# Linear attention between two mixture layers: 32 slots in a row instead of a loop of turns, x kept on chip, no identity products in front of the 64x64 groups

## The reference, cut to what matters

```python
x = x + 0.5 * ffn(layernorm(x))          # mixture layer, stage f1
x = x + linear_attention(layernorm(x))   # the part that changes
x = x + 0.5 * ffn(layernorm(x))          # mixture layer, stage f2

def step(carry, inp):                    # scan over 8 segments of 64 positions
    mem, z = carry
    q_s, k_s, v_s = inp
    sq = elu(q_s) + 1.0
    att_mem = sq @ mem / (sq @ z)
    sk = elu(k_s) + 1.0
    mem = mem + einsum('bhlk,bhlv->bhkv', sk, v_s)
    z = z + sk.sum(over the segment)
    att_dot = softmax(einsum('bhik,bhjk->bhij', q_s, k_s) * scale)
    att = gate * att_mem + (1.0 - gate) * (att_dot @ v_s)
```

## Time and profile before

| | |
|---|---|
| median of 3 runs | 2392.57 us |
| the profiled execution, its own time | 2382.67 us |
| its span, first to last instruction | 2381.0 us |
| attention stage | 844.4 to 1470.8 us |
| seven turns (b = 0 to 6), first `score` to first `score` | 70.3, 72.4, 74.9, 74.5, 72.4, 71.3, 69.0 us |
| last turn (b = 7) to the store's end | 59.1 us |

### The profile page before, as it was taken

How to read it: one execution, slowest core, us unless ns; L and a number is a source line. 1 busy time by engine, 2 the same in 40 slices (tenths; PEclk the granted TensorE clock), 3 DMA queues, 4 the chain that set the end, 5 groups by cost and what they waited for, 6 DMA issues and landing times. The chain is left out here.

```text
span 2381.0 us, 41513 instructions
## 1 busy us (share of the span) xinstructions
PE 1916.0 (80%) x12512; PEld 1065.6 (45%) x12513; DVE 1488.0 (62%) x3530; ACT 935.8 (39%) x1694; POOL 553.3 (23%) x640
## 2 busy tenths in 40 slices
PE   1899999998499958887888884599999998499940
PEld 1433333332299925565555663223333332189930
DVE  1678888884345437656666653487888886345533
ACT  0156666667222223332333321036666666322200
POOL 2222333311322231111001000222233331222246
PEclk9899999999699978888988986679999999799975
DMA  8336333320122231111011003335333330022245
GB/s 186 62 56 130 65 65 62 58 45 11 53 73 73 70 121 36 54 54 53 12 45 54 28 19 67 81 65 128 66 69 57 63 59 12 27 79 73 72 131 180
DMA packets 163076, 161.68 MB, mean 68 GB/s; under 512 B 20620, under 2 KB 153484, under 8 KB 162572
## 3 DMA queue, kind: packets, MB, share of 16 engines
q1 hardware_dynamic: 122048, 107.34, 19.7%
q10 hardware_dynamic: 30636, 27.21, 4.2%
q0 software_dynamic: 10240, 25.18, 3.7%
HBM read 90.80 MB, written 62.39 MB: 64 GB/s over the span
## 5 line engine op out<-in xcount | busy, mean ns | idle before, releaser
L576 DVE TENSOR_REDUCE f_M<-bank 128x1 f32<-128x512 f32 x1024 | 673.8, 685 | 194.0 <-PE bank L846 184.1
L486 ACT ACTIVATE f_PT<-bank 128x512 f32<-128x512 f32 x1024 | 573.0, 596 | 296.8 <-PE bank L863 292.2
L846 PE MATMUL bank<-f_KS,f_QS 96*128 96x512 bf16 x1024 | 403.8, 400 | 75.1 <-DVE f_M L576 39.1
L863 PE MATMUL bank<-f_QS,f_KS 99*128 99x512 bf16 x1024 | 394.8, 390 | 45.4 <-ACT f_PT L486 31.3
L863 PEld LDWEIGHTS bank<-f_QS,f_KS 99*128 99x128 bf16 x1024 | 99.9, 99 | 423.0 <-ACT f_PT L486 304.9
L873 PE MATMUL bank<-f_PT,f_V 128*32 128x512 f32 x2048 | 273.2, 607 | 0.0
L846 PEld LDWEIGHTS bank<-f_KS,f_QS 96*128 96x128 bf16 x1024 | 100.8, 99 | 204.8 <-DVE f_M L576 137.0
L1107 PE MATMUL bank<-f_room,f1m_gT 128*128 x568 | 136.2, 383 | 0.1
L1107 PE MATMUL bank<-f_room,f2m_gT 128*128 x568 | 135.3, 381 | 0.1
L415 POOL DMA_INDIRECT routed_rows<-f_AO,f_rows_i x128 | 124.7, 974 | 42.0 <-issue 42.0
L1107 PEld LDWEIGHTS bank<-f_room,f1m_gT 128*128 128x128 f32 x568 | 103.6, 193 | 11.8 <-issue 0.5
(11 more groups left out here) (257 smaller groups left out, 3027.4 us busy)
## 6 DMA issues: line engine op xcount, KB each, us to landing
f_QS<-q_parts SPq DMA_DIRECT2D x192, 64.0 KB
f_KS<-k_parts SPq DMA_DIRECT2D x168, 64.0 KB
expert_rows<-f1m_y ACTq DMA_DIRECT2D x71, 128.0 KB, 1.7
expert_rows<-f2m_y ACTq DMA_DIRECT2D x71, 128.0 KB, 1.7
xr<-f_xr SPq DMA_DIRECT2D x16, 512.0 KB, 3.0
f_room<-in_L_ffn_w SPq DMA_DIRECT2D x2, 4096.0 KB, 22.4
q_parts<-f_q SPq DMA_DIRECT2D x16, 384.0 KB, 2.5
k_parts<-f_k SPq DMA_DIRECT2D x16, 384.0 KB, 2.5
```

Of the source, the lines that this page charges most:

```text
L486: act.activation(PT[:, i % 8, :], SCE[i % 2][:, :], ACT.Exp).then_inc(probs_ready, 1)
L576: dve.tensor_reduce(M[:, t, h:h + 1], SCM[(a * SC + i) % 3][:, :], AX.X, ALU.max).then_inc(scm_drained, 1)
L846: pe.matmul(SCM[(a * SC + i) % 3][:, :], QS[par][0:K_MAX, h, t * P:(t + 1) * P], KS[par][0:K_MAX, h, :], start=True, stop=True).then_inc(s ...
L863: pe.matmul(SCE[i % 2][:, :], KS[par][0:K_EXP, h, t * P:(t + 1) * P], QS[par][0:K_EXP, h, :], start=True, stop=True).then_inc(sce_filled, 1)
```

## The change

- One slot per tile and no loop: 37 slots in a row (`SLOTS`), of which 4 only make the first batch's items, 32 have a tile and 1 closes; a batch is 4 slots, and its items are spread over them at four places A to D. The memory items stand with the items they need, and the last (`LATE`) in the first slot of its own batch. The layer norm of batch b+2 is made in four parts, one in each slot.
- PSUM is dealt out anew: `score` and `recall` share a pair of banks, the probabilities have two banks of their own, `OB` only the output, and the ring has 3 banks instead of 2.
- x stays in SBUF in 4 buffers: no store to `x_mid`, no load of it; `put_out` adds into the buffer.
- `carry` is gone.
- Keys are projected before queries; the gate is applied as (memory - attention) x gate + attention, with no `omg`.

Its core (the first `slot` is TensorE's, the second VectorE's):

```diff
-    PLACES = [[("hsT", 0), ("hsT", 1)], [("qk", 0), ("qk", 1)], [("qk", 2), ("qk", 3)], [("qk", 4), ("qk", 5)],
-              [("qk", 6), ("qk", 7)], [("v", 0), ("v", 1)], [("v", 2), ("v", 3)], [("sk", 0), ("sk", 1)],
...
+    PLACES = [{"A": [("hsT", 0), ("hsT", 1)], "B": [("qk", 0)], "C": [("qk", 1)], "D": [("qk", 2)]},
+              {"A": [("qk", 3), ("qk", 4)], "B": [("v", 0)], "C": [("v", 1)], "D": [("sk", 0)]},
...
-        SC, AMB, LB, OB, RING = bank[0:2], bank[2:4], bank[4], bank[5], bank[6:8]
+        SA, LB, OB, RING = bank[0:2], bank[2:4], bank[4], bank[5:8]
...
+            def slot(b, t):
+                g, before = tile(b, t), tile(b, t - 1)
+                if g is not None:
+                    score(g)
+                if before is not None:
+                    weigh(before)
+                make(b, t, "A")
+                if g is not None:
+                    recall(g)
+                make(b, t, "B")
+                if g is not None:
+                    turn_probabilities(g)
+                if before is not None:
+                    turn_out(before)
+                make(b, t, "C")
+                if before is not None:
+                    project_out(before)
+                make(b, t, "D")
...
+            def add_up(g):
-                s.own(dve.tensor_tensor(AL[:, :], LB, w["omg"][:, :], ALU.mult))
-                dve.tensor_tensor(AT[:, :], AM[:, t % 2, :], AL[:, :], ALU.add).then_inc(at_ready, 1)
+                own(dve.tensor_tensor(AT[:, :], AM[:, g % 2, :], LB[0], ALU.subtract))
+                own(dve.tensor_tensor(AT[:, :], AT[:, :], w["gate"][:, :], ALU.mult))
+                dve.tensor_tensor(AT[:, :], AT[:, :], LB[0], ALU.add).then_inc(at_ready, 1)
...
+            def slot(b, t):
+                g, before = tile(b, t), tile(b, t - 1)
+                last = ((b, t - 1) if t else (b - 1, T - 1)) if (b, t) != SLOTS[0] else None
+                if g is not None:
+                    subtract_maximum(g)
+                if last is not None:
+                    lows(*last, "D")
+                    memories(*last, "D")
+                if before is not None:
+                    add_up(before)
+                if last is not None:
+                    features(*last, "C")
+                memories(b, t, "A")
+                if g is not None:
+                    probabilities(g)
+                if last is not None:
+                    features(*last, "D")
+                lows(b, t, "A")
+                if g is not None:
+                    from_memory(g)
+                features(b, t, "A")
+                lows(b, t, "B")
+                if b + 2 < B:
+                    prepare_batch(b + 2, t)
+                features(b, t, "B")
+                lows(b, t, "C")
+                memories(b, t, "C")
+                if before is not None:
+                    put_out(before)
...
-                pe.matmul(free[:, 510:512], ident_b[:, :], ident_b[:, 0:2], start=True, stop=True)
```

More of the change, by code:

```diff
@@ L1607, in _, with score @@
             dve.wait_ge(gate_step, 2)
-            dve.tensor_scalar(w["omg"][:, :], w["gate"][:, :], -1.0, 1.0, ALU.mult, ALU.add).then_inc(gate_step, 1)
-            dve.wait_ge(gate_step, 3)
-            s = Steps(dve, dve_front, 0, FRONT)
-            for stage in (combine_rows, variance, normalise):
-                stage(0, s)
-            run_turns(dve, turn)
+            for b, t in SLOTS:
+                slot(b, t)
         @block.tensor
         def _(pe):
-            def carry(free):
-                pe.matmul(free[:, 510:512], ident_b[:, :], ident_b[:, 0:2], start=True, stop=True)
+            def score(g):
+                n = g // T
+                wait(pe, am_read, g)
+                if g % T == 0:
+                    pe.wait_ge(drained["qk"], (n + 1) * QK)
+                for h in range(H):
+                    pair, one = h // 2, h % 2
+                    part = slice(one * DK, (one + 1) * DK)
+                    for half in range(2):
+                        at = (2 * (g % T) + half) * LSEG
+                        seg = slice(at, at + LSEG)
+                        last = pe.matmul(SA[one][half * LSEG:(half + 1) * LSEG, pair * LSEG:(pair + 1) * LSEG],
+                                         qk[n % 2][part, pair, seg], qk[n % 2][part, PAIRS + pair, seg], start=True, stop=True)
+                last.then_inc(s_filled, 1)
@@ new lines, in recall @@
+            def recall(g):
+                n, t = divmod(g, T)
+                pe.wait_ge(s_ready, g + 1)
+                if t == 0:
+                    pe.wait_ge(sqk_ready, (n + 1) * QK)
+                pe.wait_ge(drained["mem"], n * U + 2 * t + 1)
+                for h in range(H):
+                    pair, one = h // 2, h % 2
+                    part = slice(one * DK, (one + 1) * DK)
+                    for half in range(2):
+                        seg = slice((2 * t + half) * LSEG, (2 * t + half + 1) * LSEG)
+                        last = pe.matmul(SA[one][half * LSEG:(half + 1) * LSEG, pair * VW:(pair + 1) * VW],
+                                         sqk[n % 2][part, pair, seg], MEM[n % 2][part, 2 * t + half, pair, :], start=True, stop=True)
+                last.then_inc(am_filled, 1)
@@ new lines, in turn_probabilities @@
+            def turn_probabilities(g):
+                pe.wait_ge(pb_ready, g + 1)
+                for half in range(2):
+                    if half == 0:
+                        wait(pe, at_ready, g)
+                    else:
+                        wait(pe, pbT_ready, g * 2)
+                    for i in range(PAIRS):
+                        last = pe.transpose(LB[half][:, i * P:(i + 1) * P], PB[g % 2][:, half * PAIRS + i, :], ident[:, :])
+                    last.then_inc(pbT_filled, 1)
@@ L1622, in turn_out, with weigh @@
+            def weigh(g):
+                pe.wait_ge(pbT_ready, (g + 1) * 2)
+                n, t = divmod(g, T)
+                for h in range(H):
+                    last = pe.matmul(LB[0][:, h * DK:(h + 1) * DK], PBT[:, (h % 2) * PAIRS + h // 2, :],
+                                     V[n % 2][:, t, h, 0:DK], start=True, stop=True)
+                last.then_inc(l_filled, 1)
             def turn_out(g):
                 pe.wait_ge(at_ready, g + 1)
+                wait(pe, y_ready, g)
@@ L1749, in _ @@
             pe.wait_ge(init, INIT)
             pe.wait_ge(la_loaded, 80)
-            run_turns(pe, turn)
+            for b, t in SLOTS:
+                slot(b, t)
 def macaron(nc, x, Wq, Wk, Wv, betas, Wo, q_w, q_b, k_w, k_b, v_w, v_b, o_w, o_b,
```

493 lines of the change are left out of this document (206 added, 287 removed), and 2 rows, old and new, of the table PLACES.

## The result

The changed kernel takes 2291.39 us (median of 4 runs, 2288.74 to 2299.78) and the one before 2391.93 (4 runs): a ratio of 0.9592, interval 0.9557 to 0.9627, about 98 us less by the ratio (the two medians are 100.5 apart). It was forecast 2326, in a range from 2284 to 2368. The sign, the range and the place of the gain were right; the gain itself was half as large again as the forecast's.

What follows compares the result with a forecast made beforehand. TensorE's work, its waits and its low clock were taken as the bound. Lead-in 26, first items 34.6, seven batches at 62.3 and last batch 69.3 made 566.0 against 626.4 us; forecast 2326, range 2284 to 2368.

Steps and rivals of the forecast that it cites:

- the last batch: Final tile slots, closing slot and store: nothing fills the waits, so 69.3 us against 59.1 before.
- Loop: Where the old loop goes back TensorE stands still: 5.5 us once, and its turns some 3 us longer.
- Identities: The 120 products ahead of 64x64 groups, 15 per batch, removed: 1.4 us a batch.
- x on chip: One store and two loads per batch become one load and one store; transfers hidden, counted 0.
- Gate: Three VectorE passes as before, but all behind `weigh`, one more than before: +0.69 us in the chain.
- The clock: Waits in third and fourth slots can lower TensorE's clock, 1.6 us a fall; 2.2 us a batch added.
- The walk: Four slots of a batch followed on the engines: 60.1 us at full clock, 52.1 work and 8.0 waits.
- Lead-in and first items: Attention's start before the seven batches: lead-in 25.0 to 26 us, first batch's items 37.4 to 34.6.
- the floor: Rival, 10%: waits shrink as products run into the next slot, clock stays up; batch 54 us, time 2268.
- The longer ring: Rival, 21%: fixed VectorE and ScalarE order lets late exponentials hold up `project_out`; batch 67 us, time 2359.
- the order that gives nothing: Rival, 6%: memories' waits are exchanged for the probabilities'; batch stays near 71 us, time 2386.
- The slower case: Rival, 7%: a wait in every slot holds TensorE's clock at half level; batch 104 us, time about 2600.

Runs made afterwards that it cites:

- x through HBM: The changed kernel with x stored to HBM and loaded back for the residual, as before the change; 2289.66 us, ratio 0.9583.
- the last kernel: The changed kernel with gate applied earlier, sum behind the probabilities, and the fourth slot's place-A memory also moved behind them; 2262.30 us, ratio 0.9492.
- the identities: The changed kernel with the identity products put back ahead of every 64x64 group; 2299.11 us, ratio 0.9615.
- the memory moved alone: The changed kernel with only the fourth slot's place-A memory addition moved behind the probabilities; 2286.99 us, one run.
- the gate earlier: The changed kernel with the memory scaled by the gate when read, leaving two VectorE passes behind `weigh` instead of three; 2289.06 us, ratio 0.9598.
- the sum behind: The changed kernel with `weigh` into `OB`, the sum's three passes behind the probabilities, and `turn_out` and `project_out` later; 2288.81 us, ratio 0.9582.
- both: The changed kernel with the gate applied earlier and the sum's passes behind the probabilities; 2280.35 us, ratio 0.9551.
- the lumped order: The changed kernel with a batch's items in their old grouping: q and k projections in two slots, v in the third; 2314.46 us, ratio 0.9690.

## Why the prediction was right, and where its sizes were off

**The mechanism** held: the gain is in the seven batches, the last batch gives some back, the waits stand at L1665 for L1518, most in the fourth and third slot, and the wait for `OB` and the loop's stop are gone. Two of the signs that it gave came out beside their bounds, both on the fast side: the wait in the third slot (1.31, forecast 1.5 to 3) and the clock of the seven batches (1.00, forecast 0.93 to 0.98).

**The edits costed singly** held. Loop: 5.5 once and some 3 in the loop's turns, measured 9. Identities: 1.4 a batch or 10 us, measured 8 on the old order and 5 to 8 on the new. x on chip: 0, measured 0 (the prediction counts one store before; the old kernel has two, `x_mid` and the result, which changes nothing in the sum). Gate: one pass more in the chain; taking it out again shortened a batch by 1.28.

**The clock** is a mis-sized term: "I add 2.2 a batch, between 0 and 2 falls in the third and fourth slots" made 15.4 us, and the profiled execution had one fall of 1.4, in the last fourth slot (15.96 instead of 14.53). It is 14 of the 33 us by which the seven batches came out shorter. By the prediction's own bounds a batch has 0 to 2 falls, and one batch in seven had one; the choice in the middle, 1.4 a batch, was not borne out. The number is not fixed by the order of TensorE's work alone: x through HBM leaves that order and its waits as they are and had two.

**The walk** is the other mis-sized term: 60.1 us a batch at full clock, measured 57.95, that is 15 us over seven. By slot it said 14.75, 14.65, 15.4 and 15.3, and measured were 14.22, 14.20, 15.00 and 14.53. In the fourth slot VectorE was to need 2.61 to the end of the difference, 3.71 for what stands between, and 2.47 for the probabilities; it needed 2.37 (to 1061.80), 3.32 and 2.34, so that TensorE could go on after 8.08 instead of 8.8. TensorE's rest of the slot, 6.5 by the walk, was 6.45. The errors of this slot are thus in VectorE, and they are of three kinds. First, 0.24 of the 2.61 was a wait for VectorE itself: in the earlier trace rows the maximum started 1.08 after `score` because a `low` stood ahead of it,

```profile
1062.07 0.43 DVE L1565 TENSOR_SCALAR la_low<-la_qk 128x512 f32<-128x512 f32 x1 [2.42 <-ACT la_qk L1399]
```

while in the inner batches of the changed kernel it starts after 0.76 to 0.90; this alone makes about 1.0 of the 2.15 us a batch in VectorE's chain. Second, durations were added up for passes that overlap by 0.08 to 0.09 where neither needs the other (0.39 in this slot). Third, the probabilities' four passes took 0.13 less; the step from the reciprocal to the product is 0.23 here and was 0.33 in the slot that was read. In TensorE two groups of 64x64 that meet take 0.91 from start to start (1104.93 to 1105.84) instead of 2 x 0.63. The first batch has in its first slot nothing of a tile before it and was 3.6 shorter, which the walk of an inner batch did not count.

**Start and end.** Lead-in and first items took 59.8 (forecast 60.6), the last batch 69.84 (69.3). That both come so near is in part luck, since their parts were off in both directions: lead-in 23.6 (26) and items 36.2 (34.6); the last batch's first slot 14.8 (12), its third 12.5 (14.5). The 566.0 forecast, less 14 for the clock, 15 for the walk, 3.6 for the first batch and 0.8 in the start, and 0.5 more at the end, gives the 533.1 measured.

**The rivals.** By the prediction's own criteria a batch (59 to 65 us for the forecast) came out below its stretch, at 57.6 on average, between the forecast and the floor of 54; TensorE's waits were 4.1 a batch, the border it gave. The measured 2291.39 lies below the forecast's own stretch (2303 to 2345), nearer to it than to the floor's 2268, and inside the range because the range reached half of the way to the floor. The floor's batch of 54 is reached by the last kernel, with the clock up as the rival said; but not by one slot's products running over into the next, rather by passes that were moved behind the probabilities. The longer ring and the order that gives nothing were excluded by the trace. The slower case, a clock at half level behind every wait, did not come; it has weaker relatives in the kernels with a fall in most fourth slots, six falls of about 1.4 us in one of them. The Trainium skill ("TensorE: Matmul & The Clock Gate", HAM oscillation) tells of a kernel in which every wait between bursts sent the clock back; its waits were for transfers, about 3 to 5 us each. The waits in the middle of the slots here are shorter and are no test of that case, so the prediction leaned on it for more than it says. What they do show is that shorter waits can be followed by a fall or not: one of 1.98 was followed by none in six of seven batches, one of 1.73 by a fall in six of seven.

## What to carry to other kernels

Walk the slot on every engine, but from start to start in rows like the ones at hand, and give passes that don't need each other the smaller step. When a wait resists, read what stands ahead of the late instruction on its own engine: here the probabilities were held by a memory that nobody needed yet, and two edits that shortened what else stood in the chain gave nothing measurable each and some 10 us together until it moved. Before a start is taken from an old trace, look whether its engine was free at that time. Value spreading of work over slots for its evenness: the same products in lumps cost 23 us, by a slot that is too full and one whose wait brings the clock down.

## What the runs showed of the hardware

- **A fall of the clock is not told by the wait's length.** The wait for the probabilities in the fourth slot was 1.98 (a fall in one of seven; with x through HBM two), 1.71 with the identities (one), 1.65 with the memory moved alone (two), 1.73 with the gate earlier (three), 1.73 with the sum behind (six), 1.73 with both (four), 3.39 in the lumped order (six, at clocks of 0.89 or 0.79 over the slot, and one without any). In the seven batches of the last kernel, with no wait over 0.52, there was none, and the second and third slots of its last batch kept a clock of 1.00 with waits of 2.06. A fall cost 1.3 to 1.7 us, in the lumped order up to 3.2. What decides is open. Within one kernel the slots are alike to a few hundredths of a microsecond up to the wait, and the clock falls in some of them only; between the kernels the products around the wait differ too, and no run here changed these alone. Nor does one trace per kernel tell how much these counts change from execution to execution.
- **The old order's clock of 0.89 cost more than loop, identities or lumps.** Without loop and identities TensorE's busy time in seven turns was 420.5 us at 0.89; in the changed kernel it is 374.9 for the same products at 1.00, 45.6 less (a part of it is pairs of 64x64 groups that meet, 0.91 instead of twice 0.63).
- **A queue in program order can make two engines wait for each other in turn**, VectorE 1.84 for a product and TensorE 1.73 for the probabilities, though the sum from which these are made had its data. Moving the one pass between them took both waits away.
- **Passes of VectorE that need nothing of each other overlap.** 128x512 float32 passes of 0.69 start 0.61 apart (1063.58 to 1064.19), and 0.72 apart where the next waits for the last (1062.14 to 1062.86).
